# Sixteen-wide attention with heads in pairs: scores for the maxima and the added maxima on the two 64-row halves of the array, one maximum for two heads

## What is computed

```python
def _L0_xattn_ref(query, key, value, w_q, w_k, w_v, w_o, b_q, b_k, b_v, b_o):
    D_K = D_MODEL // N_HEADS          # 256 // 16
    scale = jnp.sqrt(jnp.asarray(D_K, query.dtype))
    q = split_heads(query @ w_q.T + b_q)
    k = split_heads(key @ w_k.T + b_k)
    v = split_heads(value @ w_v.T + b_v)
    scores = jnp.einsum('bhqd,bhkd->bhqk', q, k) / scale
    attn = jax.nn.softmax(scores, axis=-1)
    ctx = jnp.einsum('bhqk,bhkd->bhqd', attn, v)
    out = ctx @ w_o.T + b_o
```

## Time and profile before

| what | value |
|---|---|
| time, median of 3 runs | 3731.34 us (3714.09 to 3733.42) |
| profiled execution | 3738.46 us, its span 3736.6 us |
| PE busy | 2890.6 us, 77% |
| DVE, ACT, POOL busy | 52%, 32%, 21% |
| mean granted clock of TensorE | 0.889 |
| first narrow attention | about 30 to 550 us of the span |
| second narrow attention | about 2350 to 2885 us of the span |

### The profile page before, as it was taken

The page is one execution under the profiler, slowest core; times in us unless marked ns, Lnnn a source line. Parts: engine busy times, 40 slices in busy tenths (PEclk is TensorE's granted clock), DMA queues, the critical chain, the costliest instruction groups (busy, mean ns, idle before and its releaser), DMA issues. The chain is left out here.

```text
span 3736.6 us, 50737 instructions
## 1 busy us (share of the span) xinstructions
PE 2890.6 (77%) x18646; PEld 1986.2 (53%) x18646; DVE 1960.3 (52%) x4246; ACT 1187.2 (32%) x2391; POOL 789.9 (21%) x660
## 2 busy tenths in 40 slices
PE   2899984658766799999999735489997419999980
PEld 1555542337554466666666433355554418887870
DVE  3677758975823555555555589566664301111113
ACT  0444443543530233333333334144443101111110
POOL 0445540001300111111111100044443150000005
PEclk8999997889857899999999878699999559999995
DMA  5555660010000100000000000456562121112114
GB/s 124 111 102 106 117 182 33 0 51 1 4 1 0 55 7 7 6 4 7 6 4 4 26 0 0 85 106 110 111 112 33 65 79 60 61 58 76 58 42 129
DMA packets 169950, 200.49 MB, mean 54 GB/s; under 512 B 24064, under 2 KB 145696, under 8 KB 169760
## 3 DMA queue, kind: packets, MB, share of 16 engines
q1 hardware_dynamic: 163616, 181.13, 20.8%
q0 software_dynamic: 6144, 16.79, 1.4%
HBM read 137.58 MB, written 60.29 MB: 53 GB/s over the span
## 5 line engine op out<-in xcount | busy, mean ns | idle before, releaser
L1442 POOL TENSOR_TENSOR L2x_halves_sum<-L2x_probs 128x512 f32<-128x512 f32 x128 | 163.3, 1275 | 933.2 <-ACT L2x_probs L1456 933.2
L3380 PE MATMUL L3f_pY<-L3f_W,L3f_hT 128*128 128x256 f32 x1184 | 271.6, 389 | 0.0
L3372 PE MATMUL L3f_pH<-L3f_xgT,L3f_W 128*128 128x256 f32 x1184 | 263.5, 381 | 0.8 <-ACT L3f_xgT L3391 0.8
L1137 DVE TENSOR_REDUCE L3x_mx<-L3x_pS 128x2 f32<-128x512 f32 x256 | 171.0, 687 | 158.0 <-PE L3x_pS L1258 157.8
L3380 PEld LDWEIGHTS L3f_pY<-L3f_W,L3f_hT 128*128 128x128 f32 x1184 | 229.6, 197 | 31.6
L1137 DVE TENSOR_REDUCE L0x_mx<-L0x_pS 128x2 f32<-128x512 f32 x256 | 170.9, 687 | 138.7 <-PE L0x_pS L1258 138.5
L3372 PEld LDWEIGHTS L3f_pH<-L3f_xgT,L3f_W 128*128 128x128 f32 x1184 | 226.2, 191 | 32.2 <-issue 1.2
L1023 ACT ACTIVATE L3x_probs<-L3x_pT 128x512 f32<-128x512 f32 x256 | 151.4, 597 | 267.9 <-PE L3x_pT L1274 267.6
L1023 ACT ACTIVATE L0x_probs<-L0x_pT 128x512 f32<-128x512 f32 x256 | 151.1, 600 | 254.9 <-PE L0x_pT L1274 254.6
L1000 POOL TENSOR_TENSOR L3x_halves<-L3x_probs 128x512 f32<-128x512 f32 x128 | 165.0, 1289 | 258.2 <-ACT L3x_probs L1023 257.5
L1000 POOL TENSOR_TENSOR L0x_halves<-L0x_probs 128x512 f32<-128x512 f32 x128 | 164.6, 1290 | 231.3 <-ACT L0x_probs L1023 230.6
(11 more groups left out here) (563 smaller groups left out, 6424.0 us busy)
## 6 DMA issues: line engine op xcount, KB each, us to landing
L0x_k_stack<-L0x_k_parts_dram SPq DMA_DIRECT2D x128, 128.0 KB, 4.8
L3x_k_stack<-L3x_k_parts_dram SPq DMA_DIRECT2D x128, 128.0 KB, 4.8
L3f_W<-in_L3f_W SPq DMA_DIRECT2D x16, 1024.0 KB, 7.5
L0x_q_stack<-L0x_q_parts_dram SPq DMA_DIRECT2D x32, 384.0 KB, 5.8
L3x_q_stack<-L3x_q_parts_dram SPq DMA_DIRECT2D x32, 384.0 KB, 6.1
tokens_by_expert<-zero_row SPq DMA_DIRECT2D x1, 10496.0 KB, 36.5
L3f_xg<-tokens_by_expert SPq DMA_DIRECT2D x38, 256.0 KB, 2.7
expert_outputs<-L3f_y SPq DMA_DIRECT2D x37, 256.0 KB, 2.2
```

The lines of the kernel that those rows point to most:

```text
L1137: nc.vector.tensor_reduce(mx[:, :, i], pS[n % 2][:, :].rearrange("p (j s) -> p j s", j=TB), AX.X, ALU.max).then_inc(max_done, 1)
L1442: nc.gpsimd.tensor_tensor(halves_sum[n % 2][:, :, :], probs[n % 2][:, :, 0, :], probs[n % 2][:, :, 1, :], ALU.add).then_inc(halved, 1)
L3372: ins = nc.tensor.matmul(pH[c % 4][:, 0:TILE], W1[par][:, kc, c * P:(c + 1) * P], xgT[:, kc, :], start=kc == 0, stop=kc == KC - 1)
L3380: ins = nc.tensor.matmul(pY[j][:, 0:D], hT[:, c, j * P:(j + 1) * P], W2[par][:, c, :], start=c == 0, stop=c == HCH - 1)
```

## The change

Heads go in pairs, of which the first has its rows 0 to 63 of the stack in use and the second its rows 64 to 127 for the scores that only feed the maxima. For that the order of terms differs between the heads of a pair (`Q_TERMS` and `K_TERMS` have two tables), so that each half holds the terms with the largest parts. The restack loads are cut by that parity: 16 for k and 7 for q, each with runs of 4 heads where there were 8. `pS` is one tile of two banks, written for both heads and reduced by one operation of twice the size. The maxima are added by 64-row matmuls, one on each half. The order of heads within a quad changes (`ORDER`). The function also moved in the file, so that its line numbers differ.

```diff
-    Q_TERMS = ((0, 3, 0), (3, 3, 0), (6, 2, 0))
-    K_TERMS = tuple((t, 1, part) for t, part in enumerate((0, 0, 0, 1, 1, 1, 2, 2)))
-    STACK_DMAS = len(Q_TERMS) + len(K_TERMS)
+    E2 = 2
+    NP = H // 2
+    ORDER = (0, 2, 1, 3)
+    Q_TERMS = (((0, 3, 0), (3, 3, 0), (6, 2, 0)), ((0, 2, 0), (2, 2, 1), (4, 1, 0), (5, 3, 0)))
+    K_TERMS = (((0, 3, 0), (3, 3, 1), (6, 2, 2)), ((0, 2, 2), (2, 3, 1), (5, 3, 0)))
+    STACK_DMAS = sum(len(terms) for terms in Q_TERMS) + 2 * 8
...
-    S_SLOT = [i * 14 // H for i in range(H)]
+    S_SLOT = [i * 14 // NP for i in range(NP)]
...
-        pS, pT, pO, pM = ([ps(f"{n}{i}") for i in range(2)] for n in ("pS", "pT", "pO", "pM"))
+        pS = ps("pS", (P, 1024))
+        pT, pO, pM = ([ps(f"{n}{i}") for i in range(2)] for n in ("pT", "pO", "pM"))
...
+            def load_q(b):
+                for f, terms in enumerate(Q_TERMS):
+                    for first, count, part in terms:
+                        src = q_dram[b % 2][:, part:part + count].rearrange("c t (d f e) s -> f (t d) c (e s)", d=DH, f=E2)
+                        dst = q_stack[b % 3][first * DH:(first + count) * DH, :, :]
+                        sp.dma_start(dst.rearrange("p (c f e) s -> p c f (e s)", c=CH, f=E2)[:, :, f, :], src[f])\
+                          .then_inc(stacks_in[b % 3], 16)
...
-                load(k_stack[b % 3], k_dram[b % 2], K_TERMS[:5], b)
+                load_k(b, (0,))
                 sp.wait_ge(q_split, b + 1)
                 save(q_parts, q_dram[b % 2], q_saved)
-                load(k_stack[b % 3], k_dram[b % 2], K_TERMS[5:], b)
+                load_k(b, (1, 2))
                 sp.wait_ge(q_saved, 16 * (b + 1))
-                load(q_stack[b % 3], q_dram[b % 2], Q_TERMS, b)
+                load_q(b)
...
-            def maximum(b, i):
-                n = H * b + i
-                dve.wait_ge(s_ready, n + 1)
-                nc.vector.tensor_reduce(mx[:, :, i], pS[n % 2][:, :].rearrange("p (j s) -> p j s", j=TB),
-                                        AX.X, ALU.max).then_inc(max_done, 1)
+            def maxima(b, pair):
+                n = NP * b + pair
+                dve.wait_ge(s_ready, 2 * (n + 1))
+                nc.vector.tensor_reduce(mx[:, :, :, pair].rearrange("p j u -> p u j"),
+                                        pS[:, :].rearrange("p (u j s) -> p u j s", u=E2, j=TB), AX.X, ALU.max)\
+                  .then_inc(max_done, 1)
...
+            def scores(b, pair):
+                n = NP * b + pair
+                if pair == 0:
+                    pe.wait_ge(stacks_in[b % 3], 16 * STACK_DMAS * (b // 3 + 1))
+                if n:
+                    pe.wait_ge(max_done, n)
                 for j in range(TB):
-                    ins = nc.tensor.matmul(pS[n % 2][:, j * S:(j + 1) * S], q_stack[b % 3][:, hd, j * P:(j + 1) * P],
-                                           k_stack[b % 3][:, hd, :], start=True, stop=True)
-                ins.then_inc(s_ready, 1)
+                    for u in range(E2):
+                        rows, hd = slice(u * P // 2, (u + 1) * P // 2), head_of(E2 * pair + u)
+                        ins = nc.tensor.matmul(pS[:, (TB * u + j) * S:(TB * u + j + 1) * S],
+                                               q_stack[b % 3][rows, hd, j * P:(j + 1) * P], k_stack[b % 3][rows, hd, :],
+                                               start=True, stop=True)
+                        if j == TB - 1:
+                            ins.then_inc(s_ready, 1)
...
+            def scores_T(b, pair):
+                n = NP * b + pair
+                if pair == 0:
                     bank, m = place["mT", b]
                     pe.wait_ge(free[bank], m + 1)
-                if n >= 2:
-                    pe.wait_ge(p_ready, n - 1)
+                if n:
+                    pe.wait_ge(p_ready, E2 * n)
                 for j in range(TB):
+                    for u in range(E2):
+                        hd = head_of(E2 * pair + u)
+                        nc.tensor.matmul(pT[u][:, j * S:(j + 1) * S], k_stack[b % 3][:, hd, j * P:(j + 1) * P],
+                                         q_stack[b % 3][:, hd, :], start=True, stop=False)
+                    for u in range(E2):
+                        rows = slice(u * P // 2, (u + 1) * P // 2)
+                        ins = nc.tensor.matmul(pT[u][:, j * S:(j + 1) * S], sel[rows, pair, :], mT[b % 2][rows, :],
+                                               start=False, stop=True)
+                        if j == TB - 1:
+                            ins.then_inc(t_ready, 1)
...
-                    if 0 <= r < B:
-                        score_T(r, h)
+                    if 0 <= r < B and h % E2 == 0:
+                        scores_T(r, h // E2)
```

844 lines of the change are left out of this document (417 added, 427 removed).

## The result

The changed kernel takes 3825.92 us (median of 4 executions, 3822.64 to 3830.26) against 3731.57 us for before (3714.09 to 3733.42): ratio 1.0296, 95% interval 1.0247 to 1.0344, 94 us slower. The direction was forecast and the time lies in the range; the loss is more than twice the 39 us that the sum gave. The profiled execution took 3822.64 us, its span is 3820.9 us.

A forecast was written before the change was run, and what follows sets the result against it. Bound by PE's order and the slightly longer restack chain. Rounds 0.9 us longer (23 us), rounds at either end (8) and lower clock (8) sum to 39: profiled 3738.5 becomes 3777, stated as 3770 us, range 3706 to 3860.

The forecast's parts named there:

- Two loops of nearly equal length: Kernel before: PE's order, 27.75 to 28.06 us a round, and the restack chain (q fill to next start), about 28.9.
- A pair of transposed scores: On PE: four full and four half-height matmuls with three exposed height changes take 0.95 us, against 0.87 before.
- Fills: On PE: 1.73 us a fill; some four more changes of height outside the pairs, 0.4 us a round.
- Third pair's wait: PE waits for the exp of head 3, behind take_q on ACT: 2.0 us, taken as 1.5 in stage two.
- Sixth pair's wait: PE's scores of pair 5 wait for the maxima of pair 4: 0.95 us, with one maximum taken as 1.2.
- 29.7 us a round, 29.2 in the second stage: Length of PE's order after the change, new waits included, against 28.06 us before.
- The chain of 29.8 us: Restack chain after the change: 28.9 us, plus 0.6 for later saves, plus 0.3 for the added loads.
- The cost of twelve more loads: Restack loads, 11 to 23 a round: taken as 0.3 us a round, upper bound 16 us a round.
- I add 1.7 us in five rounds, 8 us: Charge for PE's lower clock after the new 2.0 us stall: 1.7 us in five rounds, 8 us in all.
- faster: Rival: restack lands sooner and PE gaps are under half those charged; 0.9 us less in 26 rounds, 3705 us; chance 0.15.
- No change: Rival: half-height weight loads are covered, PE's path drops to 27.3 us, chain 28.9 to 29.4; 3725 to 3745 us; chance 0.20.
- Much slower: Rival: each load has a cost of its own, 4 us in 30 rounds; 3850 us or more; chance 0.10.

The follow-up runs named there:

- e7: Changed kernel with transposed scores by head at full height, scores of pairs 5, 6 and 7 in slots 9, 11 and 13; ratio 1.0171 to the kernel before.
- e8: Changed kernel with transposed scores by head, slots 0, 1, 2, 4, 6, 8, 10, 12, normalize one head sooner; ratio 1.0181 to the kernel before.
- e10: e8 with five of the k loads issued from ACT in slots 7 to 11 instead of SP's queue; ratio 1.0063 to the kernel before.
- e11: Changed kernel with transposed scores by head at full height, previous group's division at heads 3 and 4, not 5 and 6; ratio 1.0176 to the kernel before.
- e12: e11 with five of the k loads issued from ACT in slots 7 to 11; ratio 1.0035 to the kernel before.
- e3: Changed kernel with scores for the maxima and the maxima by head again, transposed scores still in pairs; ratio 1.0167 to the kernel before.
- e4: Changed kernel with the maxima added by full-height 128-row selection matmuls, all pairs kept; ratio 1.0170 to the kernel before.
- e5: Changed kernel plus 12 matmuls with overwritten output before the third pair and before the sixth pair's scores; ratio 1.0202 to the kernel before.
- e1: Kernel before with only the 23 half-size restack loads in place of its 11; ratio 1.0072 to the kernel before.

## Why the prediction came out as it did

- **Two loops of nearly equal length: right.** e7, e8, e10, e11 and e12 turn on the restack chain, e3, e4, e5 and the changed kernel on PE's order.
- **A pair of transposed scores: right.** Forecast 0.95 us, measured 0.98 (338.42 to 339.40), gaps of 0.10 to 0.11 at each change of height and none between half-height groups. e4 prices the three changes inside the pairs: 1.0 us a round. The row-group rule of the Trainium skill (TensorE: Matmul & The Clock Gate, Part 3) agrees with these gaps, but not alone: full-height matmuls share all their rows and still follow each other after 0.109 us without a gap.
- **Fills: too small.** A fill followed by another shape takes 1.93 us to the next instruction (333.10 to 335.03), not 1.73. Four fills are 0.8 us; the sum had 0.4 for changes outside the pairs.
- **Third pair's wait: right.** 1.85 against 2.0 in the first stage, 1.37 against 1.5 in the second.
- **Sixth pair's wait: mis-sized.** The maximum took 1.223 us (forecast 1.2), but the wait was 1.53 us in the first stage and 2.14 in the second, against 0.95. The kernel before already had 1.1 us there. In the second stage the scores of the fifth pair were there at about 2706.1, but DVE was still at the division (DVE of the changed kernel):

```profile
2707.22 0.42 DVE L1989 SCALAR_TENSOR_TENSOR L3x_oT<-L3x_pO,L3x_ln_sum 128x256 f32<-128x256 f32 x1
2707.57 1.22 DVE L1965 TENSOR_REDUCE L3x_mx<-L3x_pS 128x4 f32<-128x1024 f32 x1
```

  I had looked at what the reduction costs and not at what stands ahead of it. The early division of e11 confirms it: 1.97 to 0.24.
- **"29.7 us a round, 29.2 in the second stage": the first step that failed.** At the upper clock a round takes 31.4 us in the first stage (e5) and 31.2 in the second, 1.7 and 2.0 too many. Of the 2.0 the maxima's wait is 1.2, the fills 0.4 and a wait of 0.34 for mT most of the rest. Over 26 rounds e5 is 57 us longer than the kernel before, where the sum had 23.
- **The chain of 29.8 us: right in size, 29.7 in the mean of the first stage, partly by luck**, and not the bound. Its first two terms were each later than forecast (k saved at 10.9, not 10.05; q loads at 22.0 to 23.2, upper end 21.9) and the landings were faster (2.3 us for a load of k instead of 4.8). The cost of twelve more loads, taken as 0.3 us a round, is 0.1 to 0.6 by e1; the bound above of 16 us was far off. The Trainium skill (DMA: Bandwidth & Descriptors, Measured) calls transfers under 64 KB dominated by descriptors. The loads of k stand at that edge, and no loss of that kind shows on this path; the issue in SP's queue does (e10).
- **"I add 1.7 us in five rounds, 8 us": the second step that failed, by as much.** The clock costs 35 to 43 us (e5). The price was about right: a round of the first stage with two low stretches takes 34.2 us against 31.4, some 1.4 us for each. The number was wrong: the changed kernel spends 106 us at the lower level in the two windows of the table, the kernel before 11. The prediction itself says that the new wait of 2.0 us comes in every round and is "just of that size" at which the clock fell in the earlier trace rows; from that follow 26 rounds and not five, 44 us, and with the sum's other terms 3807 us.
- **The sum, term by term.** Rounds 57 us against 23, the rounds at either end 9 against 8, the clock 43 against 8: 110 us in the two stages against 39. Work that the change does not touch ran 25 us faster in this pair of profiles. The medians give 94.
- **A slip that nothing hangs on.** The 2.7 MB of the loads in the rival "faster" are too many: eight loads of 128 KB and three of 384 KB are 2.2 MB, 128 GB/s in the 17.4 us.
- **The rivals.** "No change" and "faster" fell on the PE gaps, as weighed. "Much slower" was near in size (3850) and wrong in cause: the loads cost 0.1 to 0.6 us a round (e1), not 4.

What stays open: what decides whether the clock falls. The length of the wait does not decide it alone. In e4 the same wait of 2.18 us with the same work around it lost the upper level in 5 of 13 rounds and kept it in 8; in the second stage of the changed kernel waits of 2.14 us did both too; e12 kept it after 2.17 and lost it after 1.90. Only in the first stage of the changed kernel was it lost in every round at both waits (1.85 and 1.53 us, from 171 us on). Where in time the waits fall, and the height of the matmuls around them, may matter; no run changes either alone.

## What to carry to other kernels

When a change puts a new wait into every round of a PE-bound stage, count the rounds and charge each with the idle time and with the slower work behind it; a wait that is filled with work thrown away can be cheaper. When two loops are nearly equal, a shorter PE order moves the wait to the head of the other loop: what counts is where the wait then stands, and one in front of the instruction that feeds the chain lengthens the chain itself. Where a pair of heads shares its buffers, the turn-taking that hid ACT and DVE is gone; look for what else stands in their queues, not only for the operation itself.
